# Order of the four pairs of chunks inside a round, in the last stage of a two-layer block on one core

## The reference, cut to what matters

```
alpha = softmax weights of the 8 best of 64 slots per token
si    = (alpha^T x) / sum(alpha)                     # slots gather tokens
r, z, n = gates of si and the initial slots           # GRU: sigmoid, sigmoid, tanh
S_new = (1 - z) * n + z * S
attn  = softmax(q k^T / sqrt(32)) ; y = LN(S_new + attn v)
x     = x + (alpha (y wvp + bvp)) wo + bo             # tokens read slots
```

## Time and profile before

| | |
|---|---|
| three timed runs | 950.89, 950.91, 948.59 us; median 950.89 |
| the profiled execution | 949.56 us, span 948.3 us |
| PE, DVE, ACT, POOL busy over the span | 96%, 84%, 84%, 58% |
| instructions | 25812 |

### The profile page before, as it was taken

The page is one execution under the profiler, slowest core; times in us unless marked ns, Lnnn a source line. Parts: engine busy times, 40 slices in busy tenths (PEclk is TensorE's granted clock), DMA queues, the critical chain, the costliest instruction groups (busy, mean ns, idle before and its releaser), DMA issues.

```text
span 948.3 us, 25812 instructions
## 1 busy us (share of the span) xinstructions
PE 912.3 (96%) x8641; PEld 731.9 (77%) x8641; DVE 792.3 (84%) x3563; ACT 794.2 (84%) x2162; POOL 548.7 (58%) x670
## 2 busy tenths in 40 slices
PE   8999999999999999999999999999999999999887
PEld 7899989898999989873325888877877777775566
DVE  6766998989898989989997666768889899896985
ACT  6999989898988888867875999987788888886876
POOL 4444636465565646451796147767798888891051
PEclk9999999999999999999999999999999999999999
DMA  9100000000000000000227899821000001000002
GB/s 376 67 2 2 2 2 2 2 2 2 2 1 2 2 2 2 2 2 0 89 107 201 279 305 310 296 93 35 24 15 23 24 14 25 24 3 2 1 1 89
DMA packets 36226, 57.70 MB, mean 61 GB/s; under 512 B 3456, under 2 KB 27264, under 8 KB 35712
## 3 DMA queue, kind: packets, MB, share of 16 engines
q1 hardware_dynamic: 36096, 56.07, 17.6%
HBM read 40.85 MB, written 11.01 MB: 55 GB/s over the span
## 4 chain that ended last, share of the span: by engine, by line
PE 54%; DVE 19%; ACT 7%; POOL 4%; issue 4%; DVEq 0%; ACTq 0%; POOLq 0%
PE PB L270 5%; PE PB L271 4%; PE PB L272 4%; PE PB L2151 4%; PE PB L437 3%; PE PB L2168 3%; PE PB L390 3%; PE PB L459 2%; PE PB L2123 2%; PE PB L1433 2%; PE PB L1435 2%; PE PB L1434 2%; DVE W L400 2%; ACT W L409 2%; DVE HFXT L607 1%
## 5 line engine op out<-in xcount | busy, mean ns | idle before, releaser
L409 ACT ACTIVATE W<-W,small 128x128 f32<-128x128 f32 x384 | 149.1, 392 | 13.2 <-DVE small L400 12.4
L421 POOL TENSOR_TENSOR W<-W,small 128x512 f32<-128x512 f32 x96 | 100.7, 1053 | 100.2 <-DVE small L415 100.1
L270 PE MATMUL PB<-RR_s 128*128 128x256 f32 (+1 forms) x468 | 151.5, 324 | 5.5 <-DVE RR_s L471 3.8
L271 PE MATMUL PB<-RR_s 128*128 128x256 f32 (+1 forms) x468 | 139.9, 299 | 0.0
L272 PE MATMUL PB<-RR_s 128*128 128x256 f32 (+1 forms) x468 | 139.7, 298 | 0.0
L2139 POOL TENSOR_TENSOR AR_s<-AR_s,small 128x512 f32<-128x512 f32 x128 | 129.9, 1045 | 15.4 <-DVE small L2132 15.4
L2132 DVE CUSTOM_DVE_ANT_0 AR_s<-PB,W 128x128 f32<-128x128 f32 x512 | 111.3, 287 | 2.1 <-PE PB L2123 0.3
L1409 DVE TENSOR_TENSOR RR_s<-AR_s,RR_s 128x512 fp32r<-128x512 f32 (+1 forms) x96 | 67.6, 711 | 40.4 <-ACT RR_s L1402 35.9
L270 PEld LDWEIGHTS PB<-RR_s 128*128 128x128 f32 x468 | 88.8, 190 | 15.1 <-DVE RR_s L471 6.4
L400 DVE CUSTOM_DVE_ANT_0 W<-PB,W 128x128 f32<-128x128 f32 x384 | 86.0, 282 | 13.6 <-PE PB L390 12.8
L349 DVE COPY AR_s<-PB 128x512 f32<-128x512 f32 x128 | 84.7, 682 | 13.2 <-PE PB L272 13.1
(11 more groups left out here) (461 smaller groups left out, 2634.0 us busy)
## 6 DMA issues: line engine op xcount, KB each, us to landing
RR_s<-W1D SPq DMA_DIRECT2D x13, 512.0 KB, 4.3
RR_s<-W2D SPq DMA_DIRECT2D x13, 512.0 KB, 4.8
W<-in_w SPq DMA_DIRECT2D x1, 5895.5 KB, 24.8
RR_s<-XD SPq DMA_DIRECT2D x46, 128.0 KB, 3.0
XD<-RR_s SPq DMA_DIRECT2D x18, 256.0 KB, 3.6
HQ<-W1D SPq DMA_DIRECT2D x6, 512.0 KB, 4.3
HQ<-W2D SPq DMA_DIRECT2D x6, 512.0 KB, 5.0
HQ<-XD SPq DMA_DIRECT2D x22, 128.0 KB, 3.1
```

The costliest lines, as they stand in the source:

```text
L270: nc.tensor.matmul(out, lh, rh, start=True, stop=False)
L271: nc.tensor.matmul(out, ll, rh, start=False, stop=False)
L409: e = nc.scalar.activation(SS[r][:, hl], SS[r][:, hl], ACTF.Exp, bias=mx[r][:, h:h + 1], scale=-1.0, accum_out=rc[r][:, h:h + 1])
L421: nc.gpsimd.tensor_tensor(s3, s3, over(rc[r], 2, [128, 4, 128]), ALU.mult).then_inc(s_nrm, 1)
```

## The change

From the fifth round on (r = 4 and above) the four pairs are taken in falling order, the youngest pair's step first. The generator feeds PE, ACT, DVE, POOL and the plan of the banks, so all of them change together. Which step is in which round does not change, nor do the entries between the steps, nor the order in which SP stores.

```diff
             for r in range(20):
                 for what, c in ROUNDS.get(r, [("steps", r)]):
                     if what == "steps":
-                        for n in range(4):
+                        for n in range(4) if r < 4 else (3, 2, 1, 0):
                             if 3 <= r - BEGIN[n] + 3 < 18:
                                 yield "step", n, r - BEGIN[n] + 3
```

## The result

The changed kernel takes 955.38 us (median of 6 runs, 954.56 to 956.65), the kernel before 950.85 in the same session (948.59 to 951.51): ratio 1.0053, 95% interval 1.0042 to 1.0064. It is slower, by more than the 0.3% that a measurement can tell, and 0.8 us above the range. The profiled executions are 955.87 us (span 953.6) and 949.56 (span 948.3), and the one before lies low among its runs: the difference of the profiles is 6.3, that of the medians 4.5.

The account below looks back on a forecast made before the run. No engine binds everywhere: DVE and ACT take turns early, ACT leads in the middle, PE binds at the end. Sum: 949.56 + 1.25 (end on PE) + 1.2 (stores) = 952.0 us, 8-in-10 range 949.0 to 954.6.

Parts of the forecast that it names:

- Round 4: DVE idles 1.4 us until the first addition at 902.1; its round ends at 906.3, 1.65 us late.
- Rounds 5 to 7: DVE makes up most of the delay and ends pair 3's step 7 at 915.3, 1.8 us ahead of before.
- Costed at nothing: PSUM banks, POOL's moved work, turn copies on ACT and table loads: no cost.
- Rounds 7 to 10: ACT sets the pace and idles 0.9 us, to 922.7, because 0:11 runs on DVE ahead of 3:9.
- Rival B: End of round 8: DVE's step 11 holds ACT the full 2.1 us, everything after 1.2 later, 953.2; chance 0.18.
- 3:13 and the tail: Pair 3's step 13 starts on PE at 934.8, 1.4 us early; 11.8 us of PE work follow, last copy +1.25.
- The stores: At the end, five stores leave without a gap at 0.95 us each: +1.2 us, bounds 0 and 1.3.
- A: Rival: the 1.4 us lead of pair 3's step 13 is kept to the end, 947.9 us; chance 0.08.
- C: Rival: the order does not matter, rounds are bound by an engine's sum and stores hide each other, 949.6; chance 0.12.

Follow-up runs that it names:

- fills' pair: POOL's two operations of steps 7 and 8 replaced by two fills each, in the changed kernel (952.41 us) and in the kernel before (948.98 us).
- fall_store_order: Changed kernel with SP waiting for the chunks in the order 0, 2, 1, 4, 3, 6, 5, 7: 955.42 us, ratio 1.0049 to before.
- fall_to13: Changed kernel with falling order in rounds 4 to 12 only, rising again from 13 on: 955.21 us, ratio 1.0041 to before.
- fall_memset: Changed kernel with POOL's two operations of steps 7 and 8 replaced by two fills each: 952.41 us, ratio 1.0014 to before.
- fall_from8: Changed kernel with rising order in rounds 4 to 6 and falling only from round 7 on: 957.66 us, ratio 1.0074 to before.
- rise_memset: Kernel before, in rising order, with POOL's two operations of steps 7 and 8 replaced by two fills each: 948.98 us, ratio 0.9985.

## Why the prediction was wrong, step by step

**Round 4, right.** 1.39 us of idle DVE before L2814 at 902.06, forecast 1.4 at 902.1.

**Rounds 5 to 7, the step that failed.** The prediction has "DVE now has no other wait over 0.2 us until 913.8" and each of its instructions at 0.6 to 0.8 us. DVE's waits were small, but its instructions were not: 1.57, 1.77 and 1.44 us for three of them, each held off by POOL. Lengths were taken from rows of before, and there, where the two met in L2820 and L2872, DVE had started first. The price is 2.95 us at 3:13 and at the last copy, and 2.30 at the end. Nor did "Costed at nothing" ask what POOL's work runs beside in its new place; it asked only who needs its result. With the blocks taken away the same step is near: 3:7 done at 14.90, forecast 14.98. Held against its partner with fills, the lead is 16.26 - 14.90 = 1.36 us, forecast 1.8.

**A follow-on, not foreseen.** The clock fell after PE's second wait of 1.70 us for DVE, that behind the second block. It is 0.76 of the 2.95.

**Rounds 7 to 10, right in kind.** ACT waits 1.11 us for L2833, forecast 0.9. Rival B needed 2.1 and did not occur. Pair 0's exponentials of 0:9 start 13.04 after the anchor with fills, forecast 12.98, and 15.02 in the changed kernel.

**3:13 and the tail.** The forecast lead of 1.4 became a delay of 2.3 (2.24 by the clock of the traces, 2.31 from the anchor). Without the blocks it is a lead of 0.6. PE's tail was forecast at 11.8 us, from 934.8 to 946.6; it is 10.65 from 938.40 to 949.05, so the forecast was 1.15 too long. (Its 947.2 for the last copy is also 1.29 after 945.91, not 1.25.) One reason is in the rows: before, a set of output matmuls and one of transposes took 1.23 us (941.82 to 943.05); in the changed kernel two sets of each in a row take 2.11 (942.60 to 944.71), not 2.46. In the fills' pair this and the smaller lead offset each other: +0.95 at the last copy, forecast +1.25.

**The stores, right in kind, a little small.** +1.2 forecast; 3.86 - 2.39 = +1.47 measured, and 4.50 - 2.38 = +2.12 in the fills' pair. The rate is the better part: 286 GB/s, which is 0.92 us for 256 KB, against 0.95 taken from the rows of before. (The 0.95 is a slip: 256 KB here are 262,144 bytes, which at 269 GB/s take 0.97, and the upper bound becomes 1.4.) The upper bound of 1.3 was too tight: the last seven copies run from 944.38 to 949.74, within 5.4 us, so more than five stores press on each other. The Trainium skill's DMA: Bandwidth & Descriptors, section Specifications, puts a core's limit near 358 GB/s; the 0.4 us estimated from it would have been further off, as the stores of the changed kernel reach 293 GB/s in their fastest microsecond (947 to 948).

**The rivals.** A is out: 3:13 came late, and in the fills' pair, where it came 0.64 us early, nothing of that was kept at the end. C is out: even without the blocks the falling order costs 3.07 us. The sum: 2.45 forecast, 0.62 more for the order alone (3.07), and 2.30 for the blocks at the end make 5.37. The medians differ by 4.5. The 5.37 comes from the one trace that has the first block; fall_store_order, the same work without it, ends at 52.56, +4.58. That fits the medians, but how often the first block occurs in the runs that were only timed is not known. By the medians, less exact than the traces, the order alone costs 3.4 and the blocks 4.5 - 3.4 = 1.1; so about half of what went beyond the forecast is the blocks, and the other half is the smaller lead and the larger stores' term.

**The range.** Its upper end is added up wrongly. 953.2 + 0.1 + 0.5 is 953.8, and with the 1.3 us by which the profile lies under the median it is 955.1, not 954.6. The measured 955.38 lies above that too. The step that failed is not this sum but the blocks: by the traces the order alone adds 3.07 us, and 949.56 + 3.07 = 952.6 lies well inside the range.

## What to carry to other kernels

When work is only reordered, its lengths are not constants. Check each DVE instruction that reads its large inputs from SBUF alone, in its new place, against what POOL does at that moment and which of the two starts first: here the one that came second waited for the other. Give the engine off the critical path the second place. And with strictly ordered queues, moving a young item ahead makes everything old behind it wait for the young one's input; each turn of the order here, early or late, cost more than the lead it bought.

## What the runs showed that had not been expected

- DVE and POOL hold each other off for whole instructions. A DVE instruction of 0.68 us took 1.44 to 1.77 and ended 0.54 us after POOL's end; POOL's L2872 went from 1.04 to as much as 1.60 (fall_to13). POOL's fills (0.53 us each) held nothing off, and DVE instructions with an input from PSUM were not held off. The Trainium skill's SBUF — State Buffer, section Who interferes with whom, says the same of an exclusive lock on a shared port pair, and that write-only GpSimd work stays clear of it: the traces agree in both.
- Which of two instructions that start within 0.01 us of each other gets in is not settled by the program: it went either way in traces of the same rounds, for DVE in four of five, worth 0.85 us.
- The same wait of 1.70 us on PE was followed by full clock once (911.20) and by half clock the next time (915.06). Two useless matmuls in it held the clock up.
- Left open: why the falling kernels need 3.86 to 3.94 us from the last copy to the end in five cases and 4.50 and 4.54 in two (fall_memset, fall_from8). In fall_memset the first and the last copy lie 7.9 us apart, as in the changed kernel. What sets these two apart is one issue of a store on SP: the longest took 1.49 and 1.51 us in them, 0.56 in the changed kernel and at most 1.0 in the other falling tails. Why is not known. A version faster than the kernel before was not found; rise_memset, at 0.9985, leaves work out.
